# Four blocks of a 12-block network: layer 2's cross attention as two lanes per context, the early norms applied on ScalarE, and the turned scores issued ahead of the turn of the maxima

## The reference

```python
x = x + _L0_xattn_ref(_layernorm(x), ctx, ...)      # L0x
x = x + _L0_attn_ref(_layernorm(x), ...)            # L0a: linear attention and a feed-forward
x = x + _L0_ffn_ref(_layernorm(x), ...)             # L0f: 16 experts
x = x + _L1_xattn_ref(ctx, _layernorm(x), mask, ...) # L1x
x = x + _L1_attn_ref(_layernorm(x), ...)            # L1a: 16-head softmax attention, 64 keys
x = x + _L1_ffn_ref(_layernorm(x), ...)             # L1f
x = x + _L2_xattn_ref(_layernorm(x), ctx, ...)      # L2x: 16 heads of width 8, 128 keys
x = x + _L2_attn_ref(_layernorm(x), ...)            # L2a
x = x + _L2_ffn_ref(_layernorm(x), ...)             # L2f: attention and experts
x = x + _L3_xattn_ref(_layernorm(x), ctx, ...)      # L3x: 16 heads of width 8, 128 keys
x = x + _L3_attn_ref(_layernorm(x), ...)            # L3a
x = x + _L3_ffn_ref(_layernorm(x), ...)             # L3f: experts
```

## Time and profile before

| | us |
|---|---|
| median of 3 runs (3009.4 to 3019.45) | 3016.06 |
| the profiled execution, its own time | 3007.17 |
| its span, first to last instruction | 3005.9 |
| PE busy | 2475.7 (82%) |
| DVE busy | 1931.9 (64%) |
| ACT busy | 1224.0 (41%) |
| POOL busy | 724.4 (24%) |
| mean granted TensorE clock | 0.906 of full |

### The profile page before, as it was taken

How to read it: one execution, slowest core, us unless ns; L and a number is a source line. 1 busy time by engine, 2 the same in 40 slices (tenths; PEclk the granted TensorE clock), 3 DMA queues, 4 the chain that set the end, 5 groups by cost and what they waited for, 6 DMA issues and landing times.

```text
span 3005.9 us, 65105 instructions
## 1 busy us (share of the span) xinstructions
PE 2475.7 (82%) x28016; PEld 1708.2 (57%) x28016; DVE 1931.9 (64%) x5138; ACT 1224.0 (41%) x1857; POOL 724.4 (24%) x644
## 2 busy tenths in 40 slices
PE   5788988776777987667788888888888887899999
PEld 2555556555555554444667666666655555556665
DVE  6877877676565786677766555554556655666543
ACT  2343333444333226666424434432424544544322
POOL 3322425443111320000012222221100021345343
PEclk8899999899879999798999989987879978899999
DMA  3001323000000010000000000000001000022133
GB/s 113 7 1 35 86 61 85 13 20 6 3 2 5 1 54 12 2 12 1 9 14 16 16 16 16 16 21 21 19 20 43 7 2 1 1 76 60 49 92 92
DMA packets 50465, 84.70 MB, mean 28 GB/s; under 512 B 9536, under 2 KB 24768, under 8 KB 49792
## 3 DMA queue, kind: packets, MB, share of 16 engines
q1 hardware_dynamic: 50176, 80.53, 9.8%
HBM read 77.89 MB, written 2.62 MB: 27 GB/s over the span
## 4 chain that ended last, share of the span: by engine, by line
PE 55%; DVE 21%; ACT 12%; issue 7%; POOL 5%; DMA 0%; SPq 0%; DVEq 0%; POOLq 0%; ACTq 0%
PE psum L831 4%; PE psum L798 4%; PE psum L802 4%; PE psum L401 3%; PE psum L1433 3%; PE psum L2030 2%; PE psum L1443 2%; PE psum L1791 2%; PE psum L1527 2%; DVE c_L3x_most L1568 1%; PE psum L2051 1%; PE psum L1239 1%; ACT c_L2x_p L1826 1%; PE psum L569 1%; ACT c_L2x_p L1824 1%
## 5 line engine op out<-in xcount | busy, mean ns | idle before, releaser
L786 POOL TENSOR_TENSOR c_L3f_h<-c_L3f_h,c_L3f_spread 128x512 f32<-128x512 f32 x96 | 122.1, 1304 | 111.0 <-DMA c_L3f_spread<-scratch 104.1
L821 DVE TENSOR_TENSOR c_L3f_h<-c_L3f_h,psum 128x512 f32<-128x512 f32 (+1 forms) x112 | 75.1, 683 | 87.1 <-PE psum L802 77.7
L1791 PE MATMUL psum<-constants_held,c_L2x_p 128*128 128x128 f32 x512 | 86.6, 325 | 53.1 <-ACT c_L2x_p L1826 53.0
L831 PEld LDWEIGHTS psum<-weights,c_L3f_h 128*128 128x128 f32 (+1 forms) x896 | 108.6, 195 | 17.9 <-issue 15.5
L1791 PEld LDWEIGHTS psum<-constants_held,c_L2x_p 128*128 128x128 f32 x512 | 70.0, 167 | 83.6 <-ACT c_L2x_p L1826 76.1
L811 ACT ACTIVATE c_L3f_h<-psum 128x512 f32<-128x512 f32 (+1 forms) x112 | 64.8, 595 | 129.1 <-PE psum L798 129.0
L798 PE MATMUL psum<-c_L3f_xT,weights 128*128 128x512 f32 (+1 forms) x224 | 115.4, 604 | 2.3 <-DVE c_L3f_h L821 2.3
L802 PE MATMUL psum<-c_L3f_xT,weights 128*128 128x512 f32 (+1 forms) x224 | 114.2, 598 | 0.5 <-ACT c_L3f_h L811 0.4
L831 PE MATMUL psum<-weights,c_L3f_h 128*128 128x128 f32 (+1 forms) x896 | 112.1, 281 | 0.0
L786 POOL TENSOR_TENSOR c_L0f_h<-c_L0f_h,c_L0f_spread 128x512 f32<-128x512 f32 x64 | 79.1, 1270 | 112.7 <-DMA c_L0f_spread<-scratch 109.5
L1852 DVE TENSOR_REDUCE c_L2x_mx<-psum 128x8 f32<-128x1024 f32 x64 | 77.9, 1217 | 33.3 <-PE psum L1433 32.6
(11 more groups left out here) (622 smaller groups left out, 6938.0 us busy)
## 6 DMA issues: line engine op xcount, KB each, us to landing
c_L0f_spread<-scratch SPq DMA_DIRECT2D x64, 256.0 KB, 5.6
c_L3f_spread<-scratch SPq DMA_DIRECT2D x32, 512.0 KB, 5.7
c_L2f_spread<-scratch SPq DMA_DIRECT2D x64, 128.0 KB, 3.1
c_L3f_spread<-scratch SPq DMA_DIRECT2D x64, 128.0 KB, 5.9
c_L0x_ctxT<-ctxT SPq DMA_DIRECT2D x8, 384.0 KB, 7.9
c_L1x_ctx<-ctx SPq DMA_DIRECT2D x16, 192.0 KB, 2.4
c_L2x_ctxT<-ctxT SPq DMA_DIRECT2D x8, 384.0 KB, 3.9
c_L3x_ctxT<-ctxT SPq DMA_DIRECT2D x8, 384.0 KB, 3.8
```

The source lines that it names most:

```text
L786: nc.gpsimd.tensor_tensor(h, h, j.m["spread"][:, f, :], ALU.mult).then_inc(*j.up("mixed"))
L831: put = nc.tensor.matmul(j.psum[:, 0, k * P:(k + 1) * P], j.m["h"][0:rows, f, k * P:(k + 1) * P], j.weight("down")[0:rows, f * P:(f + 1) * ...
L1791: put = t.transpose(psum[:, n // 4, (n % 4) * P:(n % 4 + 1) * P], m["p"][:, n * P:(n + 1) * P], j.c["ident"])
```

## The change

1. **L2x in two lanes.** The main programs stop after the projections. For each half of the heads (lane 0: heads 0 to 7, banks 0 and 1; lane 1: heads 8 to 15, banks 2 and 3) there are a PE, an ACT and a DVE program of their own (new letters `m`, `n`, `x`, `y`, `w`, `z`), with semaphores of their own, so each lane has its own scores, maximum, exponent, turn, product, copy, turn back and division, and its next scores wait for its own `att` alone. The `oT` copy becomes two of 256 columns, the reciprocal and the division two each, of half width.
2. **Lane masks 2 and 3 of `kx` in L2x** move from DVE to POOL (two 128x1024 TENSOR_TENSOR per job).
3. **The bias into x** in L1a, L2x and L3x moves from DVE to POOL (`pool_bias`).
4. **Early norms**: DVE computes, instead of the normed tile, `shift = -mean * rstd` (one small operation per norm), and a new early ACT program (letter `k`) applies `Identity(x * rstd + shift)`, one ACTIVATE per tile. The second norms inside L0a and L3a stay on DVE.
5. **`pe_waves`**: the turned scores of groups 1 to 3 are issued in the step after the scores, as soon as the maxima are taken from the banks (`part`), ahead of the turn of the maxima.
6. **`ORDER` is another string** throughout (8896 letters in place of 8576, with the new letters). `PLAN` is the same.

The diff, cut to its core:

```diff
@@ dve_early_norm, act_norm (early norms) @@
+def dve_early_norm(nc, j, i, x, room="norm"):
...
+    v.tensor_scalar(root[:, 0:n], moments[:, 0:n, 1], 1.0, LN_EPS, ALU.mult, ALU.add).then_inc(*j.up("variance"))
+    yield
+    dve_shift(nc, j, i, shift[:, 0:n], moments, root[:, 0:n])
+
+def dve_shift(nc, j, i, shift, moments, root):
+
+    nc.vector.wait_ge(*j.at("rstd", i))
+    nc.vector.scalar_tensor_tensor(shift, moments[:, :, 0], -1.0, root, ALU.mult, ALU.mult).then_inc(*j.up("shift"))
+
+def act_norm(nc, j, i, out, x, root, shift):
+
+    nc.scalar.wait_ge(*j.at("shift", i))
+    for t in range(x.shape[1]):
+        put = nc.scalar.activation(out[:, t, :], x[:, t, :], ACT.Identity, bias=shift[:, t:t + 1], scale=root[:, t:t + 1])
+    put.then_inc(*j.up("normed"))
@@ pe_waves @@
         pe_scores(nc, j, w, keys)
         yield
+        t.wait_ge(*j.at("part", 4 * w + 1))
+        pieces = [(u, r) for u in range(tiles) for r in range(2)]
+        for u, r in pieces:
+            for g in (1, 2, 3):
+                pe_turned_scores(nc, j, w, keys, g, u, r)
+        yield
         t.wait_ge(*j.at("max", w + 1))
...
-        yield
-        pieces = [(u, r) for u in range(tiles) for r in range(2)]
-        for u, r in pieces:
-            for g in (1, 2, 3):
-                pe_turned_scores(nc, j, w, keys, g, u, r)
@@ pool_bias @@
+def pool_bias(nc, j, bias):
+
+    j.begin(nc.gpsimd)
+    nc.gpsimd.wait_ge(*j.at("normed", 1))
+    nc.gpsimd.tensor_tensor(j.x, j.x, bcast(j.weight(bias), 1, j.tiles), ALU.add).then_inc(*j.up("biased"))
@@ pe_lane_L2x @@
+            for r in range(2):
+                s = 2 * w + r
+                for g in groups:
...
+            put.then_inc(*j.up(lane_name("scores", h)))
+            yield
+            t.wait_ge(*j.at(lane_name("exp", h), w + 1))
+            for n in range(8 * h, 8 * h + 8):
                 put = t.transpose(psum[:, n // 4, (n % 4) * P:(n % 4 + 1) * P], m["p"][:, n * P:(n + 1) * P], j.c["ident"])
+            put.then_inc(*j.up(lane_name("p_turned", h)))
             yield
+            t.wait_ge(*j.at("pT1" if h else "pT0", w + 1))
+            for g in groups:
...
+            put.then_inc(*j.up(lane_name("out", h)))
+            yield
+            t.wait_ge(*j.at(lane_name("outT", h), w + 1))
...
@@ act_lane_L2x @@
+            s.wait_ge(*j.at(lane_name("low", h), w + 1))
+            s.activation(p, p, ACT.Relu, scale=-1.0).then_inc(*j.up(lane_name("e_low", h)))
+            s.wait_ge(*j.at(lane_name("e_low", h), w + 1))
+            s.activation(p, p, ACT.Exp, scale=-WIDTH ** -0.5).then_inc(*j.up(lane_name("exp", h)))
...
+            s.copy(m["oT"][:, 0, 256 * h:256 * h + 256], psum[:, 2 * h, 0:256]).then_inc(*j.up(lane_name("outT", h)))
@@ pool_L2x @@
+    g.wait_ge(*j.at("k_ready", 1))
+    for n in (2, 3):
+        put = g.tensor_tensor(m["kx"][:, n, :], m["kT"][:], j.c["lane4"][:, n:n + 1].to_broadcast([P, 8 * SC]), ALU.mult)
+    put.then_inc(*j.up("kx"))
+    yield
+    pool_bias(nc, j, "bo")
@@ ORDER @@
-    "DDdvDVddlLDdqQqQppddDDdaPapaggAGlPApppvDPAvdavPPLGPvVVAvVVDVVDdddppaapagglDDvdPAppPpAQqPALGGPPPvvavvVVvAppVaapaVdddVDDvD"
+    "DVDvddQqDLpdDKldDkqQdDddDLapDKaglPpAaPApPpAGgGpvvdPPaPVVkAvvvVVVppaPgapPvdddDVlAagppApDdvDvPGAPPavvLGPVVAkvvqQpagpapaVDV"
```

404 lines of the change are left out of this document (228 added, 176 removed).

## The result

The changed kernel takes 3038.75 us (median of 20 executions, 3016.56 to 3059.21). The kernel before, timed beside it, takes 3013.03 us (20 executions, 2991.26 to 3025.66). The ratio is 1.0096, with a 95% interval from 1.0075 to 1.0117: **slower by 1%**, where 1.2% faster was forecast. The measured time lies outside the range. The profiled execution took 3058.18 us, near the slow end of its runs, so single stages of it are read with some 20 us of doubt. What follows rests on the ratios of the experiments first, and on single traces where several of them agree.

The account below looks back on a forecast made before the run. No engine was taken as the bound, but two jobs' dependence chains through engines in fixed order. Terms -28 - 2 - 3 - 4 + 3 - 3 = -37 us from 3007.2 gave 2970, median 2979 us; 8-in-10 range 2925 to 3022.

Parts of the forecast that it names:

- the one on POOL: Start of L2x jobs: kx lanes 2 and 3 moved to POOL, net -2 us, ends +10 and -12.
- 4 x 2.5 = +10: L2x: kx split between DVE and POOL is ready 2.6 us later, counted once in each of four rounds.
- a gain of 12: L2x job start: first half of a first wave no longer waits for the second's work, about 3 us per round.
- -4 us for the bias: L1a, L2x, L3x: 24 additions of 0.69 us leave DVE for POOL; -4 us, ends -5 and +5.
- The sign that was to warn: L2x: kx on POOL over 3 us each, with long waits of the scores, would sink the second term.
- The lanes: -28 us: L2x in two lanes: wave pace from 8.7 to 7.7 us, -28 us, ends 0 and -48.
- The norms: -3 us: Early norms moved from DVE to ACT: 31 us leave the chain, 23 and 5 return; ends -31 and +20.
- rival A: Slower: norms waiting for shift hold ACT's queue, +53 us, median 3032 us; chance 0.14.
- the 100 us that were to sink the forecast: ACT's waits for shift summing to 100 us or more would show the slower rival right.
- The turned scores: -3 us: L1a and L3x: turned scores ahead cover the split maxima; -3 us, ends -17 and +10.
- Rival B: Hardly any change: L2x keeps its pace of 8.7 us per wave, sum -9, median 3007 us; chance 0.19.
- Rival C: Clearly faster: lanes close PE's gaps in L2x and its clock rises, -22 us, median 2957 us; chance 0.17.

## Why the prediction was wrong

**The step that failed is the one on POOL.** "Per round of two jobs I count it once: 4 x 2.5 = +10." Against that it set a gain of 12, which made -2 us, and it took -4 us for the bias. The mechanism was seen in the earlier trace rows, and then counted against a gain that was only argued.

Measured, kx costs 22 or 32 us, by which of the two is taken back first, the bias 9 or 19, both together 41. The hold-up itself was priced well: 2.6 us for a round's first job, 2.05 measured, and 2.4 us per round with the second job, 10 us in all. What failed is what was made of it. The gain of 12 us at the start of the job did not come: in the run with kx on DVE the stretch between rounds is 26 us, 21 to 30 before. The price on the path was left at the length of the hold-up, when it is more than twice that, for two reasons that the sum had at nothing. Two operations that PE waits for stand behind the held one on DVE, `va` (13.3 us where it was 6.2) and the other context's addition into `x` (8.0 where it is 4.1 with kx on DVE). And PE's own work in the stage takes 16 us longer (268.9 against 252.4) at a clock of 0.88 instead of 0.94.

For the bias it was not asked what of DVE runs beside it; it is the kx operations of the other context. The sign that was to warn, `kx` on POOL over 3 us each, looked at the wrong engine: POOL's take 2.1, it is DVE's that take 2.0 where they took 0.79. By the rule of the Trainium skill that the prediction named (GPSIMD Engine Reference, section 8, Key points) the part alone was +10, which has the right sign.

**The lanes: -28 us, measured -12.** Alone, in the old order, they are worth 12 us. The pace was right for two rounds of four, which take the 54 us that were forecast at a higher clock than before; the other two take 62.3 and 64.1. With kx on DVE, in the new order, the whole stage is 20 us shorter than before, in the change 4 us longer. Not seen was that a lane's half of the scores costs PE as much time as the whole did (1.09 us for 8 records, about 1.1 to 1.3 for 16), which is 27 us more on an engine that was called no bound.

**The norms: -3 us, and rival A.** The tile takes 0.41 us, not 0.3, so ACT got 223 us, not 163. The sum itself was wrong: 31 us of 150 is a fifth, but the terms that come back were divided by six, and 163 / 6 is 27, not 23. By a fifth the part would have been +8. In the new order they wait 80 us for `shift` in all, under the 100 us that were to sink the forecast, and the change is 0.6% slower without them; A is not what happened. But A is real: in the old order the same operations cost 5.4%.

**The turned scores: -3 us.** In their own order they are worth 1.2%, 36 us; in the old one they cost 1.5%, 46 us. The new wait that was foreseen came (5.6 us for the copied maxima in L3x), with another that was not (9.4 us for the first maxima). The 25 us more of PE time were not foreseen. They are no price of this part alone: behind the turn it is still 87.1 us in the change's order, and in the change with kx and bias on DVE, which has the same order of PE, 80.6. The granted clock over most of L3x is 0.80 in the change (2091 to 2420 us) and 0.94 in that run (2066 to 2375).

**The sum.** Everything but POOL's part was forecast at -31 us. It measures -12 (0.9960; by the interval -5 to -19). POOL's part was forecast at -6 and measures +41. Their sum is +29, and 0.96% of 3013 is +29. Rival B's picture, a pace that stays, is wrong for the two middle rounds and right for the stage. Rival C's is seen in part: when the hold-up is gone, the clock in L2x is 0.93 or 0.94 instead of 0.88. The chance of 0.14 for slower hung on A alone; the mishap that came had a term but no case.

What stays open: how much of the -12 us is owed to the norms, the turned scores and the new order, each of which only makes sense with the others; how the bias on POOL comes to cost what it does; and where in L1a to L3x the 27 us and 45 us of new PE time come to lie on the path.

## What to carry to other kernels

Before an operation goes from DVE to POOL to relieve DVE, look at what DVE runs at that moment: here it was an SBUF-to-SBUF TENSOR_SCALAR, and splitting four operations between the two engines took 4.8 us where DVE alone needed 2.7. Then look at what stands behind it on DVE, for both contexts: the stage lost more than twice what DVE was held. A cheap test is a spare copy of POOL's operation into a tile that nobody reads. In a kernel with an order written out, a part and its order are one change: parts taken alone gave up to 5.4% in the wrong direction, so undo a part in the new order and add it in the old before either is believed.

## What the runs showed of the hardware that was not expected

- Matmuls of 32 rows and 64 columns that are issued together took the time of one: 1.07 us for 4 records, 1.09 for 8, 1.11 or 1.12 for 16 in most waves. Split in two batches that were issued apart they took about twice that.
- DVE's TENSOR_SCALAR of 128x1024 in SBUF takes 0.68 to 0.75 us alone and up to 2.49 us beside a POOL TENSOR_TENSOR, which itself takes 1.89 us and, with a DVE operation in between, 2.34. Beside ACT's operation of the same size DVE's stays at 0.75.
- The time of one and the same kernel goes with its mean granted clock: in four series of 17 to 29 executions of the kernel before, 0.891 to 0.912, it falls by 16 to 20 us for each 0.01 (in one series 3027 us at 0.893, 2993 at 0.912). The change has a mean of 0.902, the change with kx and bias on DVE 0.911. By that slope, an estimate, some 17 of the 41 us between them came with the clock.
- An ACTIVATE of 128x128 with a scale and a bias from SBUF takes 0.48 us, and in groups of four one starts each 0.41 us.
